# Paired attend steps in a masked attention, and cell edge projections placed ahead of the scores

## The chip, the cores and the metric

One core of one Trainium2 chip. The metric is the device time of one execution of the whole program, in microseconds (us). Before the change it is 3072.13 us, the median of three runs (3067.86 to 3075.75). Some 0.3% is what a measurement of this kernel can tell from no change.

## The reference, cut to what matters

The program takes `x`, 64 batches of 64 tokens by 256 features (4096 tokens), and runs six residual stages on it:

```
x = x + xattn0(layernorm(x), ctx, ctx, mask)     # "masked attention", 16 heads of 16
x = x + attn0(layernorm(x), context)             # "wide attention", 8 heads of 128, 1024 keys
x = x + ffn0(layernorm(x))                       # "cell": six nodes, each an attention
x = x + xattn1(layernorm(x), ctx)
x = x + attn1(layernorm(x))                      # a scan
x = x + ffn1(layernorm(x))
```

The change touches the first and the third. The masked attention projects queries from the normalised tokens, keys and values from the 256 context rows of each batch, closes masked keys, and takes a softmax over 256 keys per head. The cell computes six nodes in turn:

```
for c in range(6):
    q = ew[c,0] * (node[c-1] @ We[eq] + be[eq])          # the edge
    k = ew[c,1] * (node[snode] @ We[ek] + be[ek])
    v = ew[c,2] * (node[middle] @ We[ev] + be[ev])
    node[c] = act_w[c] * mha(q, k, v, Wq[c], Wk[c], Wv[c], Wo[c]) + q
out = layernorm(node[5])
```

Its attention has 8 heads of 32 and runs over the 64 tokens of one batch. Only node 0's value source (for node 1) is the node just computed; from node 2 on keys and values come from older nodes.

## The kernel before, in words

Every stage is a block in which each engine has its own instruction stream; a semaphore is raised by one engine and waited for by another. The order of the work is written out by hand: the functions named `body` list what each engine does in a unit, in order, and an engine never passes an instruction that waits.

**Masked attention** (`stage_masked_attention`, L447). 32 units of 128 tokens, that is two batches `b`, in a loop over two units (`units`, L545). A unit has 8 steps `t` (`STEPS`), each a pair of heads of one batch; the first four belong to batch 0, the last four to batch 1. Per unit PE does: `turn_probs(u, t)` (L750, matmuls L759) for all eight steps, into the one PSUM bank `turn`, so turn t waits until turn t-1 is copied; `scores` (L733, L745) for batch 1 of this unit and for batch 0 of the next; `attend(u, k, j)` (L762, L774) four times, j = 0 to 3, each from two steps' turned probabilities, tiles of 128*32; and for the next unit `project_q` (L690), `project_k` twice (L699, L709), `project_v` twice (L713, L722), plus `project_o` (L726) of the unit before and `turn_x` (L682) of the unit after the next. Its order (L778 to L819) is: turn 0, attend 3 of the unit before, queries, turn 1, scores batch 1, turn 2, attend 0, keys, turn 3, keys, turn 4, attend 1, output, turn 5, scores of the next unit, turn 6, attend 2, values, turn 7, values, turn_x.

Softmax: DVE adds the mask and finds the row minimum (`find_min`, L967), ACT takes the exponential with its row sum (`exp`, L883), DVE inverts the sum (`invert`, L1019), POOL multiplies (`scale_probs`, L637), PE turns, and ACT or DVE copies the turned block into `probT` (`copy_turned`, L892 and L977), which holds four steps, so the copy waits for an attend of the same unit. Every product of projections and scores is taken in three passes of high and low parts: ACT rounds the high part (`split_ctx` L859, `copy_q` L867, `copy_k` L872), DVE takes the low part (`ctx_lo` L981, `q_lo` and `k_lo` L984). POOL also normalises the tokens two units ahead (`inverse_std` L615, `normalise` L622 to L624), spreads the queries (`spread`, L629) and adds the bias (L643). DVE's `pick` (L1010, L1013) gathers the attended heads, `finish` (L1024) adds the output.

**Cell** (`stage_cell`, L1769). Four rounds `i`, each with two blocks of 512 tokens, the inputs X = 0 and 1. A round has twelve attentions: node c = 0 to 5, and for each X = 0, then 1. Attention number a = 12 i + 2 c + X. The PE order of one attention (L2192 to L2241) is: `add_edge(0, ...)` (first half of the edge projection, 6 matmuls of 512 columns into the bank `acc[0]`, L2137), `turn_late` (L2120, probabilities 2 and 3), `add_edge(1, ...)`, `attend` (L2148), keys of the next node for this X (L2063; in c = 0 only half of them here, in c = 5 `turn_input` L2052 instead), `add_output` (L2159), `turn_early` of the *other* input's probabilities 0 and 1 (L2112), values (L2086), queries (L2063 into `ring`), scores (L2101). So the scores of one X are computed while the other X is attended next.

DVE per attention (L2516 to L2557): for the four score banks row maximum and subtraction (L2465, L2468); in X = 0, after two of them, `split_fused` (L2412), the low part of the next fused weights, 128x1536; low part of the attended rows (L2413); sums, inversion and division of the probabilities (L2473, L2479, L2483); low part of the node (L2413); in X = 1 the low part of the own weights (`split_own`, L2449); in c = 3 and 4 the normalisation of the next round's input, in c = 5 `finish`, the last layernorm and the residual (L118 to L143, L2500, L2503). ACT copies turned probabilities, takes exponentials, rounds attended rows, keys, node, values and queries, splits the weights' high parts (L2266, L2271) and issues the loads of the next weights and the stores (`store`, L2330), each store waiting for `finish`. One semaphore, `set_lo`, counts both kinds of low weight parts. POOL in this stage only takes inverse square roots (`gpsimd_rstd`, L127).

## Time and profile before

| | |
|---|---|
| median of three runs | 3072.13 us (3067.86 to 3075.75) |
| the profiled execution | 3063.59 us, its span 3061.9 us |
| PE busy | 2868.9 us (94%) |
| DVE busy | 2214.2 us (72%) |
| ACT busy | 2050.7 us (67%) |
| POOL busy | 1104.2 us (36%) |
| first and last score matmul of the masked attention | 23.5 and 564.0 us |
| first and last edge matmul of the cell | 1632.7 and 2594.7 us |

A row of a timeline gives the start (us from the span's start), the length, the engine, the line, the operation with output<-inputs, the tile shape and operand shape of PE, and how many instructions were merged (x24). In brackets stands the idle time of the engine before the row and who ended it. Lengths of PE rows overlap a little, because matmuls are pipelined: the distance from start to start is what a group costs. "issue" is idle time for which the profile shows no other engine.

### The profile page before, as it was taken

Reading aid. Unit: us, or ns where it says so; the run is one execution under the profiler, and the core shown is the slowest. Engines: PE = TensorE matmul, PEld = TensorE weight load, DVE = VectorE, ACT = ScalarE, POOL = GpSimd, SP = SyncE. Lnnn points to the kernel's source line nnn. Section 1 sums busy time; section 2 is a strip of 40 time slices with the busy share of each in tenths; the row PEclk is TensorE's granted clock in tenths of the full one; section 3 lists DMA queues with packets and bytes.
Section 4 is the critical chain, followed back from the end, with each engine's and each line's share of the span. In section 5 each row is a group of like instructions: output and inputs, shape, how many; then the busy total and the mean of one; then the engine's idle time right before and its main releaser. Section 6 shows DMA issues by size and latency. Waiting matters only on the chain. (4 is left out here: it accounts for less than half of the span.)

```text
span 3061.9 us, 84828 instructions
## 1 busy us (share of the span) xinstructions
PE 2868.9 (94%) x32198; PEld 2227.6 (73%) x32198; DVE 2214.2 (72%) x5367; ACT 2050.7 (67%) x4144; POOL 1104.2 (36%) x939
## 2 busy tenths in 40 slices
PE   7999999789999999999979999999999998788899
PEld 6777777556666666666667887887887787566798
DVE  7888888777777767777637788788778776668543
ACT  6888888687777777787706766666676665333444
POOL 6777777476665555665600000000000000111210
PEclk9999999999999999999989999999999999899899
DMA  4111111077899888898961112111011110651000
GB/s 147 50 58 50 58 48 48 9 134 136 152 159 148 151 149 151 151 160 144 196 235 43 37 43 71 37 44 57 34 44 50 50 37 26 204 166 58 8 21 28
DMA packets 620992, 275.15 MB, mean 90 GB/s; under 512 B 548972, under 2 KB 593959, under 8 KB 620471
## 3 DMA queue, kind: packets, MB, share of 16 engines
q1 hardware_dynamic: 600726, 226.96, 35.0%
q10 hardware_dynamic: 19968, 44.05, 4.2%
q8 instruction: 208, 3.41, 0.5%
q14 instruction: 90, 0.73, 0.1%
HBM read 115.21 MB, written 21.50 MB: 45 GB/s over the span
## 5 line engine op out<-in xcount | busy, mean ns | idle before, releaser
L1334 POOL TENSOR_TENSOR front_parts<-wide_prob,front_parts 128x1024 f16<-128x1024 f32 x256 | 546.3, 2135 | 351.9 <-ACT front_parts L1555 278.8
L1653 DVE TENSOR_REDUCE wide_row_max<-wide_score 128x1 f32<-128x1024 f32 x256 | 312.6, 1221 | 130.0 <-PE wide_score L1375 129.8
L1543 ACT ACTIVATE wide_prob<-wide_score,wide_neg_max,wide_s_up 128x1024 f32<-128x1024 f32 x256 | 307.6, 1202 | 146.6 <-DVE wide_neg_max L1656 139.4
L1375 PE MATMUL wide_score<-wide_kT,wide_qT 128*128 128x512 f16 x1536 | 376.8, 382 | 6.5 <-ACT wide_prob L1543 4.9
L637 POOL TENSOR_TENSOR mask_prob<-mask_prob,mask_inv_sum 128x512 f32<-128x512 f32 x256 | 271.0, 1064 | 94.7 <-DVE mask_inv_sum L1019 90.8
L883 ACT ACTIVATE mask_prob<-mask_prob,mask_row_min 128x256 f32<-128x256 f32 x512 | 255.5, 502 | 68.3 <-DVE mask_row_min L967 64.9
L1555 ACT ACTIVATE front_parts<-wide_prob 128x1024 f16<-128x1024 f32 x256 | 269.9, 1054 | 16.9 <-ACT wide_prob L1543 8.7
L1375 PEld LDWEIGHTS wide_score<-wide_kT,wide_qT 128*128 128x128 f16 x1536 | 144.8, 98 | 154.3 <-ACT wide_prob L1543 6.6
L2465 DVE TENSOR_REDUCE cell_row_max<-cell_score 128x8 f32<-128x512 f32 x192 | 131.3, 684 | 152.5 <-PE cell_score L2101 149.9
L130 POOL TENSOR_TENSOR cell_var_eps<-cell_mean_var,const_eps 128x4 f32<-128x4 f32 x8 | 1.6, 202 | 641.2 <-DVE cell_mean_var L124 641.2
L1391 PE MATMUL wide_pv<-front_probT,wide_v 128*128 128x256 f16 x1536 | 188.8, 273 | 1.8 <-DMA front_probT<-front_parts 1.8
L1391 PE MATMUL wide_turn<-front_probT,wide_v 128*128 128x256 f16 x1536 | 188.3, 273 | 2.3 <-DMA front_probT<-front_parts 2.3
L967 DVE CUSTOM_DVE_ANT_0 mask_prob<-mask_score,mask_shut 128x256 f32<-128x256 f32 x512 | 189.4, 416 | 0.0
L1391 PEld LDWEIGHTS wide_pv<-front_probT,wide_v 128*128 128x128 f16 x1536 | 150.1, 98 | 45.7 <-issue 3.3
L1391 PEld LDWEIGHTS wide_turn<-front_probT,wide_v 128*128 128x128 f16 x1536 | 150.2, 98 | 45.5 <-issue 2.5
L759 PE MATMUL mask_turn<-const_ident,mask_prob 128*128 128x128 f32 x1024 | 158.4, 277 | 16.2 <-ACT mask_probT L892 13.3
L2137 PE MATMUL cell_acc<-cell_node,cell_w 128*128 128x512 f32 x576 | 160.3, 414 | 9.9 <-ACT cell_probT L2340 6.1
L2294 ACT ACTIVATE cell_v<-cell_score 64x256 f32<-64x256 f32 x384 | 145.5, 379 | 29.1 <-PE cell_score L2086 24.6
L2086 PE MATMUL cell_score<-cell_w,cell_node 128*128 128x256 f32 x1152 | 150.9, 288 | 5.5 <-DVE cell_node L2413 4.0
L130 POOL TENSOR_TENSOR cell_last_var_eps<-cell_last_mean_var,const_eps_cell 128x4 f32<-128x4 f32 x8 | 1.6, 202 | 420.2 <-DVE cell_last_mean_var L124 420.2
L2159 PE MATMUL cell_acc<-cell_oT,cell_w 128*128 128x512 f32 x576 | 145.3, 401 | 7.5 <-DVE cell_oT L2413 7.4
L759 PEld LDWEIGHTS mask_turn<-const_ident,mask_prob 128*128 128x128 f32 x1024 | 116.5, 141 | 46.3 <-POOL mask_prob L637 30.0
(356 smaller groups left out, 6848.7 us busy)
## 6 DMA issues: line engine op xcount, KB each, us to landing
cell_w_stage<-cell_weights ACTq DMA_DIRECT2D x24, 768.0 KB, 5.2
mask_ctx<-in_ctx_turned SPq DMA_DIRECT2D x32, 512.0 KB, 3.2
ctx_ctx<-in_ctx SPq DMA_DIRECT2D x32, 512.0 KB, 4.2
cell_w_stage<-in_L_ffn_W_own ACTq DMA_DIRECT2D x24, 512.0 KB, 3.6
mask_mask<-in_mask_BxS_ik SPq DMA_DIRECT2D x32, 256.0 KB, 3.5
front_probT<-front_parts SPq DMA_TRANSPOSE x512, 3.3
cell_prob<-in_L_ffn_W_pairs SPq DMA_DIRECT2D x10, 512.0 KB, 5.5
front_x_all<-in_x SPq DMA_DIRECT2D x32, 128.0 KB, 2.1
```

Source lines behind the costliest of these rows:

```text
L637: pool.tensor_tensor(prob[:, b, two, :], prob[:, b, two, :], inv_sum[:, b, two].unsqueeze(2).to_broadcast([P, 2, CTX]), ALU.mult)\
L759: mm = pe.transpose(turn[:, (i * KT + kt) * P:(i * KT + kt + 1) * P], prob[:, b, s * 2 + i, kt * P:(kt + 1) * P], ident[:, :])
L883: ins = act.activation(prob[:, b, p, :], prob[:, b, p, :], ACT.Exp, bias=row_min[:, b, p:p + 1], scale=-1.0, accum_out=row_sum[:, b, p:p + 1])
L967: ins = dve.tensor_tensor_reduce(prob[:, b, p, :], score[p % ROW][:, p // ROW * CTX:(p // ROW + 1) * CTX], shut[:, k, b, :], 1.0, 3.4e38, ...
L1334: pool.tensor_tensor(parts[:, s % 2, LO, :], prob[:, s % 2, :], parts[:, s % 2, HI, :], ALU.subtract).then_inc(part_lo, 1)
L1375: mm = pe.matmul(score[:, s % 2, half * 512:(half + 1) * 512], qT[:, u_par, a, s * P:(s + 1) * P], kT[:, par, b, half * 512:(half + 1) * 5 ...
L1391: mm = pe.matmul(pv_banks[hf][:, :], v[:, par, a, kb, :], probT[:, u_par, hf, :, b, kb, :], start=(kb == 0 and i == 0), stop=(kb == KB - 1 ...
L1543: act.activation(prob[:, s % 2, :], score[:, s % 2, :], ACT.Exp, bias=neg_max[:, s % 2:s % 2 + 1], scale=s_up[:, 0:1], accum_out=row_sum[: ...
L1555: act.activation(parts[:, s % 2, HI, :], prob[:, s % 2, :], ACT.Copy).then_inc(part_hi, 1)
L1653: dve.tensor_reduce(row_max[:, one], score[:, s % 2, :], AX.X, ALU.max).then_inc(max_found, 1)
L2086: mm = pe.matmul(score[2 + pair][:, s * D:(s + 1) * D], v_src[:, a, ih, half(2 * pair + s)], weight(b, fused_at(2), ih, slice(0, D)), star ...
L2137: pe.matmul(acc[oh][:, :], weight(a_, EDGE_AT, ih, half(oh)), src[:, b_, ih, :], start=(j == 0 and ih == 0), stop=False)
```

## The change

Masked attention: `probT` holds all eight steps; attends 0 and 1 stand together behind turn 4, attends 2 and 3 behind turn 0 of the next unit; ACT's exp 3 moves from the end of a unit behind `split_ctx` of the next; DVE's inversions 3 and 4 and POOL's scaling 7 change places with a neighbour. Cell: the first half of the next attention's edge projection stands between queries and scores; the low part of the fused weights moves from DVE to POOL, with a semaphore of its own; at the end of the last round `finish` and `store` of block 0 move behind the attended rows of the last attention.

```diff
-    probT = mem.sb("probT", [P, PER_BATCH, 2, KT, P])
+    probT = mem.sb("probT", [P, STEPS, 2, KT, P])
...
             scale_probs(u, 6)
+            scale_probs(u, 7)
             if not last and has_second(u):
                 inverse_std(u + 2)
                 normalise(u + 2, k)
-            scale_probs(u, 7)
...
+        def attend_batch(u, k, b):
+            for j in range(b * DH, (b + 1) * DH):
+                attend(u, k, j)
...
             turn_probs(u, 0)
             if not first:
-                attend(u - 1, 1 - k, GROUPS - 1)
+                attend_batch(u - 1, 1 - k, 1)
...
             turn_probs(u, 2)
-            attend(u, k, 0)
...
             turn_probs(u, 4)
-            attend(u, k, 1)
+            attend_batch(u, k, 0)
...
             turn_probs(u, 6)
-            attend(u, k, 2)
...
         def copy_turned(u, t):
             act.wait_ge(turn_ready, u * STEPS + t + 1)
-            if t >= PER_BATCH or positive(u):
-
-                act.wait_ge(heads_ready, u * GROUPS + t // 2 - 1)
+            if positive(u):
+
+                act.wait_ge(heads_ready, (u - 1) * GROUPS + t // 2 + 1)
...
             if not last:
                 split_ctx(u + 1, 1 - k)
+            exp(u, 3)
             copy_turned(u, 1)
...
                 copy_v(u + 1, 1 - k, 1)
-                exp(u + 1, 3)
...
-            invert(u, 3)
             if not last:
                 ctx_lo(u + 1, 1 - k)
+            invert(u, 3)
             find_min(u, k, 4)
...
             find_min(u, k, 5)
+            invert(u, 4)
             if not last and has_second(u):
                 ln_stats(u + 2, k)
-            invert(u, 4)
```

The cell, on POOL, PE, ACT and DVE in this order:

```diff
+        def split_fused(number):
+            pool.wait_ge(set_hi, number * 2 + 2)
+            pool.tensor_tensor(w_set[:, LO, FUSED_AT:SET], w_stage[:, FUSED_AT:SET], w_set[:, HI, FUSED_AT:SET].bitcast(F32), ALU.subtract)\
+                .then_inc(fused_lo, 1)
+
         def body(i, last):
-            for X in range(2):
-                if not last:
-                    norm.gpsimd_rstd(pool, (i + 1) * 2 + X)
+            for c in range(NODES):
+                if not (last and c == NODES - 1):
+                    split_fused(set_number(i, c))
+                if c in (3, 4) and not last:
+                    norm.gpsimd_rstd(pool, (i + 1) * 2 + c - 3)
...
         project_v(0, 1)
+        add_edge(0, 0, 0, 0, 1, 0)
         scores(DH, 2 * 6)
...
-                add_edge(0, a, c, X, set_no, use)
+                after = (c + X) % NODES if X == 1 else c
+                after_set = set_number(i, c) + X
+
+                def edge_ahead():
+                    add_edge(0, a + 1, after, 1 - X, after_set, use)
+
+                if final and X == 1:
+                    add_edge(0, a, c, X, set_no, use)
                 turn_late(use, a, X)
...
                     if X == 0:
-                        pe.wait_ge(set_lo, set_no * 2 + 2)
+                        pe.wait_ge(fused_lo, set_no + 1)
...
                     project_q(use + Q_AT, Q_AT, c + 1, X)
+                    edge_ahead()
                     scores(use + Q_AT, proj_at(i, c, X) + PROJ_SLOT)
...
                     project_q(use + Q_AT + DH, Q_AT + DH, 0, X)
+                    edge_ahead()
                     scores(use + Q_AT + DH, proj_at(i, c, X) + PROJ_LAST)
...
                     act.activation(oT[:, HI, hf, :], ring[hf][:, :], ACT.Identity, bias=fused_bias[:, c, 2, hf:hf + 1]).then_inc(attended_hi, 1)
+                if final and X == 1:
+                    store(i, 0)
...
-                    store(i, X)
+                    if not (final and X == 0):
+                        store(i, X)
...
-                if X == 0:
-                    if not final:
-                        split_fused(set_number(i, c))
...
                     low(oT[:, LO, hf, :], ring[hf][:, :], oT[:, HI, hf, :], fused_bias[:, c, 2, hf:hf + 1]).then_inc(attended_lo, 1)
+                if final and X == 1:
+                    finish(i, 0, last)
...
-                if c == NODES - 1:
+                if c == NODES - 1 and not (final and X == 0):
                     finish(i, X, last)
```

DVE's `copy_turned` changes as ACT's does. `set_lo` is split into `own_lo` (own weights, DVE) and `fused_lo` (fused weights, POOL); all waits on it follow.

## Rows read from the trace of the kernel before

**Rows 1.** windows view, masked, then cell: stretch, length, busy PE PEld DVE ACT POOL, clock, DMA

```profile
264.00:401.00 137.00, 132.86 (x1556) 107.05 (x1553) 115.20 (x472) 118.12 (x361) 105.99 (x120) 1.00 0.16 54
1850.00:2095.00 245.00, 236.13 (x4156) 196.75 (x4155) 195.92 (x337) 168.22 (x313) 4.84 (x8) 1.00 0.14 47
```

**Rows 2.** PE's timeline in a masked unit: start us, us, engine, line, operation

```profile
307.73 0.63 PE L759 MATMUL mask_turn<-const_ident,mask_prob 128*128 128x128 f32 x4 [0.33 <-ACT mask_probT L892]
308.29 0.64 PE L774 MATMUL mask_heads<-mask_probT,mask_v 128*32 128x128 f32 x16
308.86 1.66 PE L709 MATMUL mask_ring<-mask_ctxT,mask_w_kv 128*128 128x512 f32 x6
310.36 0.60 PE L759 MATMUL mask_turn<-const_ident,mask_prob 128*128 128x128 f32 x4
310.71 1.64 PE L709 MATMUL mask_ring<-mask_ctxT,mask_w_kv 128*128 128x512 f32 x6
...
315.23 0.98 PE L745 MATMUL mask_score<-mask_kT,mask_q_diag 32*128 32x256 f32 x24 [0.18 <-DVE mask_kT L984]
```

**Rows 3.** the weight loads (PEld) of attend in the same unit

```profile
308.29 0.38 PEld L774 LDWEIGHTS mask_heads<-mask_probT,mask_v 128*32 128x32 f32 x16 [0.17 <-issue]
```

**Rows 4.** ACT's timeline in the same unit

```profile
300.10 0.51 ACT L883 ACTIVATE mask_prob<-mask_prob,mask_row_min 128x256 f32<-128x256 f32 x1 [1.48 <-DVE mask_row_min L967]
...
309.29 0.51 ACT L883 ACTIVATE mask_prob<-mask_prob,mask_row_min 128x256 f32<-128x256 f32 x1 [0.30 <-DVE mask_row_min L967]
...
317.25 0.51 ACT L883 ACTIVATE mask_prob<-mask_prob,mask_row_min 128x256 f32<-128x256 f32 x1 [1.48 <-DVE mask_row_min L967]
```

**Rows 5.** DVE's timeline in the same unit

```profile
307.14 1.42 DVE L981 TENSOR_TENSOR mask_ctxT<-mask_ctx,mask_ctxT 128x1024 fp32r<-128x1024 f32 x1 [0.78 <-ACT mask_ctxT L859]
```

**Rows 6.** PE's timeline around one attention of the cell stage

```profile
1689.14 2.91 PE L2063 MATMUL cell_ring<-cell_node,cell_w 128*128 128x512 f32 x12
1691.98 1.76 PE L2101 MATMUL cell_score<-cell_kT,cell_qT 32*64 32x64 f32 x128
1693.67 1.65 PE L2137 MATMUL cell_acc<-cell_node,cell_w 128*128 128x512 f32 x6
...
1698.90 3.06 PE L2063 MATMUL cell_score<-cell_node,cell_w 128*128 128x512 f32 x12
...
1704.60 1.03 PE L2112 MATMUL cell_ring<-const_ident,cell_prob 128*128 128x128 f32 x8
...
1708.34 2.91 PE L2063 MATMUL cell_ring<-cell_node,cell_w 128*128 128x512 f32 x12
1711.54 1.58 PE L2101 MATMUL cell_score<-cell_kT,cell_qT 32*64 32x64 f32 x128 [0.30 <-ACT cell_qT L2286]
1713.06 1.65 PE L2137 MATMUL cell_acc<-cell_node,cell_w 128*128 128x512 f32 x6
```

**Rows 7.** DVE's timeline in and after the same attention

```profile
1699.67 1.41 DVE L2413 SCALAR_TENSOR_TENSOR cell_oT<-cell_ring,cell_fused_bias,cell_oT 128x512 fp32r<-128x512 f32 x2 [0.56 <-ACT cell_oT L2347]
...
1702.58 1.29 DVE L2483 TENSOR_TENSOR cell_prob<-cell_prob,cell_inv_sum 128x512 f32<-128x512 f32 x2
...
1715.77 1.75 DVE L2412 TENSOR_TENSOR cell_w<-cell_w_stage,cell_w 128x1536 fp32r<-128x1536 f32 x1
```

**Rows 8.** ACT's timeline at the end of it

```profile
1711.87 1.48 ACT L2271 ACTIVATE cell_w<-cell_w_stage 128x1536 fp32r<-128x1536 f32 x1
```

**Rows 9.** the page, part 5: the subtraction on POOL in the wide attention

```profile
L1334 POOL TENSOR_TENSOR front_parts<-wide_prob,front_parts 128x1024 f16<-128x1024 f32 x256 | 546.3, 2135 | 351.9 <-ACT front_parts L1555 278.8
```

**Rows 10.** the waits view of PE in the cell stage: us, times, longest

```profile
PE cell_acc L2159 <- DVE cell_oT L2413: 7.4, 9, 1.5
```

**Rows 11.** the end of the cell stage, PE's and DVE's timelines

```profile
2594.73 0.79 PE L2137 MATMUL cell_acc<-cell_node,cell_w 128*128 128x512 f32 x1 [6.09 <-ACT cell_probT L2340]
...
2606.41 1.41 DVE L118 BATCH_NORM_STATS2 cell_last_stats<-cell_z 128x6 f32<-128x256 f32 x4 [6.81 <-ACT cell_z L2374]
...
2612.38 1.23 DVE L2503 TENSOR_TENSOR cell_x_res<-cell_x_res,cell_z 128x1024 f32<-128x1024 f32 x1
```

More of the change, by code:

```diff
@@ L774, in attend @@
                     mm = pe.matmul(heads[r * ROWS:(r + 1) * ROWS, hf * P:(hf + 1) * P], v[:, k, b * KT + kt, p * ROWS:(p + 1) * ROWS],
-                                   probT[:, p // 2, p % 2, kt, :], start=(kt == 0), stop=(kt == KT - 1))
+                                   probT[:, b * PER_BATCH + p // 2, p % 2, kt, :], start=(kt == 0), stop=(kt == KT - 1))
             mm.then_inc(heads_ready, 1)
+        def attend_batch(u, k, b):
+            for j in range(b * DH, (b + 1) * DH):
+                attend(u, k, j)
         def body(u, k, first, last):
@@ L837, in _ @@
         units(pe, body)
-        attend(UNITS - 1, 1, GROUPS - 1)
+        attend_batch(UNITS - 1, 1, 1)
         pe.wait_ge(y_ready, UNITS - 1)
@@ L888, in copy_turned @@
             act.wait_ge(turn_ready, u * STEPS + t + 1)
-            if t >= PER_BATCH or positive(u):
-                act.wait_ge(heads_ready, u * GROUPS + t // 2 - 1)
-            act.activation(probT[:, t % PER_BATCH].rearrange("p i k q -> p (i k q)"), turn[:, :], ACT.Copy).then_inc(turn_copied, 1)
+            if positive(u):
+                act.wait_ge(heads_ready, (u - 1) * GROUPS + t // 2 + 1)
+            act.activation(probT[:, t].rearrange("p i k q -> p (i k q)"), turn[:, :], ACT.Copy).then_inc(turn_copied, 1)
         def body(u, k, first, last):
@@ L933, in _ @@
         exp(0, 2)
-        exp(0, 3)
         units(act, body)
@@ L973, in copy_turned @@
             dve.wait_ge(turn_ready, u * STEPS + t + 1)
-            if t >= PER_BATCH or positive(u):
-                dve.wait_ge(heads_ready, u * GROUPS + t // 2 - 1)
-            dve.tensor_copy(probT[:, t % PER_BATCH].rearrange("p i k q -> p (i k q)"), turn[:, :]).then_inc(turn_copied, 1)
+            if positive(u):
+                dve.wait_ge(heads_ready, (u - 1) * GROUPS + t // 2 + 1)
+            dve.tensor_copy(probT[:, t].rearrange("p i k q -> p (i k q)"), turn[:, :]).then_inc(turn_copied, 1)
         def low(dst, src, hi):
@@ L1847, in stage_cell @@
     set_hi = mem.sem("set_hi")
-    set_lo = mem.sem("set_lo")
+    own_lo = mem.sem("own_lo")
+    fused_lo = mem.sem("fused_lo")
     biases_done = mem.sem("biases_done")
@@ L2128, in add_edge @@
                 if X == 0:
-                    pe.wait_ge(set_lo, set_no * 2 + 1)
+                    pe.wait_ge(own_lo, set_no)
             src = node[:, X, :, place(source[c][0])]
@@ L2174, in _ @@
         turn_input(0, 0)
-        pe.wait_ge(set_lo, 2)
+        pe.wait_ge(fused_lo, 1)
         pe.wait_ge(proj_copied, DH)
@@ L2234, in body @@
                     if X == 0:
-                        pe.wait_ge(set_lo, set_no * 2 + 2)
+                        pe.wait_ge(fused_lo, set_no + 1)
                     pe.wait_ge(proj_copied, proj_at(i, c, X) + DH)
@@ L2376, in body @@
                 if X == 0 and not final:
-                    act.wait_ge(set_lo, set_number(i, c) * 2 + 2)
+                    act.wait_ge(own_lo, set_number(i, c))
+                    act.wait_ge(fused_lo, set_number(i, c) + 1)
                     load_set((c + 1) % NODES)
@@ L2423, in _ @@
                     dve.wait_ge(set_hi, 2)
-                    low(w_set[:, LO, FUSED_AT:SET], w_stage[:, FUSED_AT:SET], w_set[:, HI, FUSED_AT:SET]).then_inc(set_lo, 2)
-                    dve.wait_ge(set_lo, 2)
+                    low(w_set[:, LO, FUSED_AT:SET], w_stage[:, FUSED_AT:SET], w_set[:, HI, FUSED_AT:SET]).then_inc(fused_lo, 1)
+                    dve.wait_ge(fused_lo, 1)
             dve.tensor_scalar(edge_bias[:, c, :], be[:, :, edge[c][0]], ew_sb[:, 3 * c:3 * c + 1], None, ALU.mult)
@@ L2450, in split_own @@
                                                ALU.mult, ALU.subtract)
-            ins.then_inc(set_lo, 1)
-        def split_fused(number):
-            dve.wait_ge(set_hi, number * 2 + 2)
-            low(w_set[:, LO, FUSED_AT:SET], w_stage[:, FUSED_AT:SET], w_set[:, HI, FUSED_AT:SET]).then_inc(set_lo, 1)
+            ins.then_inc(own_lo, 1)
         def input_rest(blk, X, banks=score):
```

## The prediction

> **What bounds the kernel now.** I read the windows view first, then PE's timeline in the two stages the change touches, then the timelines of the engines that feed it, then PE's waits. In the masked attention PE is busy 132.9 of 137 us [rows 1], in the cell stage 236.1 of 245 us [rows 1]: both run at the pace of PE's instruction order, and only what shortens that order, or a wait inside it, pays. What the reader should see in each: how little PE idles, and that what it does wait for comes once per unit, at a fixed place.
>
> Masked attention. One unit lasts 17.15 us, from the exp of pair group 0 at 300.10 to the same at 317.25 [rows 4]. PE waits twice in it: 0.33 us before turn 2 (for ACT's copy of turn 1) and 0.18 us before the next unit's scores (for DVE's low part of the keys) [rows 2]. So the period is a loop over three engines: turn 2 (307.73) to the next scores (315.23), 7.50 us on PE [rows 2]; scores to exp 0 (317.25), 2.02 us by scores and row minimum [rows 2, 4]; exp 0 to turn 2, 7.63 us, whose pace ACT sets, since it is ACT's copy of turn 1 that PE waits for at its end [rows 2, 4].
>
> Cell. An attention takes 19.39 us here (1693.67 to 1713.06) [rows 6]. At its end come the queries, then the scores, which wait 0.30 us for ACT's copy of the queries; the scores then take 1.52 us. Where no wait is shown before them they take 1.69 us [rows 6], so I read 0.17 us of wait for the second query half inside them.
>
> **The change in the masked attention.** (1) Attend steps go in pairs. Turn 2 to attend costs 0.56 us and attend to keys 0.57, while turn 3 to keys costs 0.35 [rows 2]; taking attend 0 out from between turn 2 and keys saves 0.56 + 0.57 - 0.35 = 0.78 us, and the same again at turn 6. It comes back as the second attend of a pair. Its price is not shown: at most 0.57 us as now, at least the 0.38 us that its weight loads run, since 0.17 us of issue idle precedes each group [rows 3]. I take 0.45, nearer the lower end, because that idle stands where the tile shape changes (128*128 to 128*32) and nothing changes between two attends. By itself: the Trainium skill (TensorEngine Tiling (Array Packing), Key Properties) says that changing the tiling mode drains the engine and changing only the tile does not; by it the second attend costs the 0.38, by the row of a single attend 0.57, which is 6 us apart over the stage. (2) On ACT split_ctx goes ahead of exp 3; both stay before the copy of turn 1, so 7.63 us stays. But DVE's low part of the context, which now waits 0.78 us for ACT [rows 5], starts up to 1 us earlier, so row minima 4 follow the scores sooner, and the 0.30 us that ACT waits for them before exp 4 [rows 4] goes. (3) The copies into the doubled probT wait for an attend of the unit before: long done. (4) Scaling 7 moves ahead of POOL's normalisation, about 2.4 us of POOL work; PE needs the latter only at the end of the unit, about 1 us later than I place it. (5) The shut-off of attend 0 and 1 until turn 4 delays the pick into oT behind DVE work that waits for exp 7 anyway.
>
> PE's part of the loop: 7.50 - 0.78 + 0.45 - 0.18 (the wait) = 6.99; the keys' low part, ready at turn 2 + 7.3, comes 0.3 to 0.5 earlier, at 6.8 to 7.0: even. Scores to exp 0 and exp 0 to turn 2 unchanged. So 0.5 us a unit; with the row minimum also freed of 0.05, and a part of the second PE gain where turn 2 waited less, 0.55. Over 31 units: **17 us**. Bounds: 0.15 us a unit (second attend at 0.57, keys' low part moved by nothing), 5 us; and PE alone, 17.15 - 0.33 - 0.18 - 2 x (0.78 - 0.38) = 15.84, 1.3 us a unit, 40 us, which the ACT part of the loop excludes up to about 0.9, 28 us. Late next: PE now waits for ACT before turn 2 by 0.5 us or more.
>
> **The change in the cell.** Edge half 0 of the next attention goes between queries and scores: no instruction added. (1) It covers the query copies. Queries and scores take 3.20 + 1.52 = 4.72 us for this input and 2.84 + 1.69 = 4.53 for the other (1689.14 to 1693.67) [rows 6]; without waits 2.84 + 1.52 = 4.36. So 0.36 us for one and 0.17 for the other, and an attention takes 19.03 us in both. 32 plain attentions (cells 1 to 4 in four rounds): 16 x 0.36 + 16 x 0.17 = 8.5 us. (2) What the cover costs: scores to turn_early of the same scores' probabilities shrinks by the 1.49 us of edge 0. From the end of scores T, the first probabilities are ready on DVE at 1702.58 + 0.65 = T + 9.56, less the 0.56 us that DVE waited for ACT [rows 7], which attend, now 1.49 earlier, removes: T + 9.0. PE wants them at 1704.60 - 1693.67 - 1.49 = T + 9.44 [rows 6]. It holds, by 0.4. That is for input 1; for input 0 DVE has the low part of the fused weights in the same stretch, 1.75 us [rows 7], and there it would be late by 1.2 us: this is what moving it to POOL pays for. (3) On POOL: 1536 columns at 2.135 us per 1024 [rows 9] are 3.2 us. ACT has the high part ready at 1713.35, T + 0.3 [rows 8]; with 1.49 - 0.36 us put in ahead of T that becomes T - 0.8. So POOL ends at T + 2.4; keys need it at 1698.90 - 1693.67 - 1.49 = T + 3.74 [rows 6]. Hidden, margin 1.3 us. (4) Losses. DVE reaches the attended low part only at 1699.11 = T + 5.44 [rows 7], first half done at T + 6.1. In cell 0 only half the keys, in cell 5 only the input's turns stand ahead of add_output, which is then wanted at T + 5.2 and T + 4.7. Today these places wait 7.4 us in all [rows 10]. By my count input 1 loses 0.65 us in seven of them, 4.5 us, input 0, freed of 1.75 us of DVE, gains 0.3 to 1.0, 4 us: even. (5) The end. The last attention's half edge waits 6.09 us for ACT, which stands at the store of block 0 and that for DVE's finish [rows 11]. Now both come after the last attended copies. But finish 0 still takes 7.2 us (2606.41 to 2613.61 for the like one [rows 11]), the store still stands on ACT ahead of the last copies, and the second finish follows. It moves from 2606.4 to about 2603.4: 3 us, between 0 and 6. Cell: 8.5 + 0 + 3 = **11.5 us**, bounds 0 (scores to turns dearer by the 0.17 of a shape change, losses 8) and 20.
>
> **A rule that speaks against it.** The POOL subtraction at L1334 takes 2135 ns on average over 256 of them, beside a DVE that works too [rows 9], so I keep 3.2 us. By itself: the Trainium skill (GPSIMD Engine Reference, Key points) says GPSIMD shares its SBUF interfaces with VectorE and contends with DVE instructions that have two SBUF inputs; by it the subtractions after T would stretch POOL's pass. This is rival C.
>
> **Sum.** 17 + 11.5 = 28.5 us off. The profiled execution took 3063.6 us (span 3061.9), so 3035 by its own time. It stands 8.5 us, 0.28%, below the median of 3072.1, and below all three runs; the result is a median, so I take 3072.1 - 28.5, rounded to 3043.
>
> **Rivals.** A: the cell gives nothing, the DVE chain (0.4 us of margin) becomes its bound and the special cells lose; for it, the margins above; against, the 0.30 us waits of PE [rows 6]. Left: 17 - 3 = 14 us, 3058. B: the masked attention stays at 17.1 us, because another engine closes the loop, POOL above all (106 of 137 us busy [rows 1]) with scaling 0 behind the normalisation; left 11 to 13 us, 3060. C, slower: POOL's pass cannot run while DVE works. Place: keys of input 0. It decides once the pass takes more than 4.3 us. DVE works from T without pause to T + 5.4; POOL, with 2.4 us left at T, would end at T + 8 at the earliest, and the keys wait 4.2 us in 23 attentions, 97 us, less 25: 3144. Against it stand the POOL rows. D: both gain more, loop 0.9 us and cell 20 us: 48 us, 3024.
>
> **How the numbers follow.** Chances: forecast 0.60, A 0.12, B 0.10, C 0.04, D 0.10, nothing at all 0.04. A measurement of this kernel can tell some 0.3%, 9 us, from no change. A and B end at 3058 and 3060, close to the bound of 3063, and I give a part of each (0.08 together) to "same", with the 0.04 and a little of the forecast's tail: faster 0.83, same 0.12, slower 0.05. The range takes in A, B and nearly D: 3022 to 3064.
>
> **What would show it.** Right: the masked unit at 16.5 to 16.7 us with PE's wait before turn 2 grown to 0.5 us and none before scores; plain cell attentions at 19.0 to 19.1 us, no wait of scores for queries, none of keys for POOL; POOL's pass at 3.2 us; the 6.09 us wait gone and the last finish 3 us nearer. Wrong: keys waiting for POOL, turn_early waiting for DVE's probabilities, scores in the masked stage still waiting for the keys' low part, or the issue idles of PE grown, as dense short instructions of scores and attend now stand 1.5 us closer.

## The result, and the profile after

The changed kernel takes 3037.99 us (median of four runs, 3034.36 to 3042.38); the kernel before, beside it, 3072.92 (3067.86 to 3075.75). The ratio is 0.9892, 95% interval 0.9878 to 0.9906; a repetition (experiment 12) gave 0.9890 (0.9874 to 0.9906). So it is 1.1% faster, 33 us by the ratio and 35 by the medians; 28.5 were forecast. The profiled execution took 3038.47 us, its span 3036.8.

PE's waits in the masked attention, then in the cell stage and the start of the one behind it (us in total, times, longest):

```profile
PE mask_turn L759 <- ACT mask_probT L894: 6.7, 15, 1.8
PE mask_score L745 <- DVE mask_kT L985: 1.7, 1, 1.7
...
PE cell_acc L2168 <- DVE cell_oT L2436: 10.5, 12, 1.5
PE cell_ring L2157 <- issue: 6.6, 10, 1.1
PE cell_ring L2179 <- ACT cell_kT L2383: 6.4, 1, 6.4
...
PE cell_score L2072 <- POOL cell_w L2012: 2.2, 3, 0.8
...
PE cell_score L2110 <- issue: 1.2, 1, 1.2
```

The masked scores no longer wait for the keys in each unit (one wait of 1.7 us is left), and the cell's scores no longer wait for ACT's queries. The 6.09 us of [rows 11] has become 6.4 us one step later, at L2179. The output projection (`add_output`, L2168) waits for DVE 10.5 us in all, after the 7.4 us of [rows 10]. And the keys wait for POOL's pass three times, 2.2 us in all, in the cells 0 of the first, second and fourth round.

PE's timeline in a masked unit, to lay beside [rows 2]:

```profile
300.44 0.63 PE L759 MATMUL mask_turn<-const_ident,mask_prob 128*128 128x128 f32 x4
300.82 1.64 PE L709 MATMUL mask_ring<-mask_ctxT,mask_w_kv 128*128 128x512 f32 x6
302.30 0.60 PE L759 MATMUL mask_turn<-const_ident,mask_prob 128*128 128x128 f32 x4
302.65 1.64 PE L709 MATMUL mask_ring<-mask_ctxT,mask_w_kv 128*128 128x512 f32 x6
304.37 0.63 PE L759 MATMUL mask_turn<-const_ident,mask_prob 128*128 128x128 f32 x4
304.93 1.08 PE L774 MATMUL mask_heads<-mask_probT,mask_v 128*32 128x128 f32 x32
305.94 1.13 PE L730 MATMUL mask_ring<-mask_wT,mask_oT 128*128 128x256 f32 x4
...
307.44 0.98 PE L745 MATMUL mask_score<-mask_kT,mask_q_diag 32*128 32x256 f32 x24
...
317.09 0.63 PE L759 MATMUL mask_turn<-const_ident,mask_prob 128*128 128x128 f32 x4
```

The unit takes 16.65 us (300.44 to 317.09) instead of 17.15; turn 2 to scores 7.00 instead of 7.50. The pair of attends (x32) costs 1.01 us, a single one cost 0.57, so the second costs 0.44. But keys to turn 4, which is 1.47 us where nothing waits, takes 302.65 to 304.37, 1.72: an unshown wait of 0.25 us (no idle under 0.15 us stands in brackets in any row of this study, and an idle inside a merged row is not shown either; the distance from start to start shows both).

The cell, to lay beside [rows 6], PE's timeline, and POOL's new pass:

```profile
1698.14 2.91 PE L2072 MATMUL cell_ring<-cell_node,cell_w 128*128 128x512 f32 x12
1700.89 1.52 PE L2146 MATMUL cell_acc<-cell_node,cell_w 128*128 128x512 f32 x6
1702.34 1.59 PE L2110 MATMUL cell_score<-cell_kT,cell_qT 32*64 32x64 f32 x128
1703.87 1.09 PE L2129 MATMUL cell_ring<-const_ident,cell_prob 128*128 128x128 f32 x8
...
1707.70 3.06 PE L2072 MATMUL cell_score<-cell_node,cell_w 128*128 128x512 f32 x12
...
1721.34 1.59 PE L2110 MATMUL cell_score<-cell_kT,cell_qT 32*64 32x64 f32 x128
```

```profile
L2012 POOL TENSOR_TENSOR cell_w<-cell_w_stage,cell_w 128x1536 fp32r<-128x1536 f32 x23 | 79.9, 3473 | 639.7 <-ACT cell_w L2290 639.7
```

Queries, edge and scores follow each other with no idle in brackets, and an attention takes 19.0 us (1702.34 to 1721.34). POOL's pass is 3.47 us on average over 23.

### The profile page after: what moved, and what is told of

The parts are those of the page before. It is cut to its first block and busy times, and to the rows that moved or that the text cites. A ratio compares the mean times of both kernels' runs of the same rounds, so it can differ in the third digit from the quotient of the medians.

```text
span 3036.8 us, 84862 instructions
## 1 busy us (share of the span) xinstructions
PE 2852.6 (94%) x32198; PEld 2229.5 (73%) x32198; DVE 2174.6 (72%) x5344; ACT 2046.2 (67%) x4144; POOL 1174.6 (39%) x962
## 5 line engine op out<-in xcount | busy, mean ns | idle before, releaser
L2012 POOL TENSOR_TENSOR cell_w<-cell_w_stage,cell_w 128x1536 fp32r<-128x1536 f32 x23 | 79.9, 3473 | 639.7 <-ACT cell_w L2290 639.7
L885 ACT ACTIVATE mask_prob<-mask_prob,mask_row_min 128x256 f32<-128x256 f32 x512 | 254.9, 502 | 47.8 <-DVE mask_row_min L968 47.5
L759 PE MATMUL mask_turn<-const_ident,mask_prob 128*128 128x128 f32 x1024 | 157.7, 277 | 15.6 <-ACT mask_probT L894 6.7
L2146 PE MATMUL cell_acc<-cell_node,cell_w 128*128 128x512 f32 x576 | 154.1, 402 | 0.7 <-ACT cell_probT L2359 0.5
L2168 PE MATMUL cell_acc<-cell_oT,cell_w 128*128 128x512 f32 x576 | 144.8, 400 | 10.5 <-DVE cell_oT L2436 10.5
L2072 PE MATMUL cell_score<-cell_node,cell_w 128*128 128x512 f32 x576 | 147.4, 402 | 2.4 <-POOL cell_w L2012 2.2
```

The costliest lines, as they stand in the source:

```text
L759: mm = pe.transpose(turn[:, (i * KT + kt) * P:(i * KT + kt + 1) * P], prob[:, b, s * 2 + i, kt * P:(kt + 1) * P], ident[:, :])
L885: ins = act.activation(prob[:, b, p, :], prob[:, b, p, :], ACT.Exp, bias=row_min[:, b, p:p + 1], scale=-1.0, accum_out=row_sum[:, b, p:p + 1])
L2146: pe.matmul(acc[oh][:, :], weight(a_, EDGE_AT, ih, half(oh)), src[:, b_, ih, :], start=(j == 0 and ih == 0), stop=False)
```

## Where the gain lies: the profiles side by side

One profile is not enough here: the wide attention, the same code in all fourteen profiles, takes 983.1 to 991.6 us from the last group of masked score matmuls to the first matmul of the cell. The first column below is a mean over four profiles whose cell stage is that of before (before, experiments 1, 3 and 4), the second over four with the changed cell stage (the changed kernel, experiments 2, 6 and 12). The times run from the scores of one attention to those of the next and are added up (16 plain attentions of each input, which are those of the cells 1 to 4 in four rounds):

| us | cell as before (4 profiles) | changed (4 profiles) | edge in place (1) |
|---|---|---|---|
| plain, input 0 | 311.3 (309.4 to 312.8) | 309.4 (308.4 to 311.0) | 310.6 |
| plain, input 1 | 319.3 (317.6 to 320.1) | 306.1 (305.7 to 306.8) | 312.5 |
| cell 0, both inputs | 175.6 | 174.9 | 171.6 |
| cell 5, both inputs, three rounds | 136.2 | 136.7 | 135.0 |
| end of the last scores to the next stage's first matmul (two profiles each) | 49.6 | 47.4 | |

Plain attentions give 15.1 us, cells 0 and 5 nothing, the end 2.2: 17 us. The ranges of input 0 overlap, and three more profiles with these attentions (experiments 5, 10 and 11) give it 308.5 to 312.1 us, so that only the gain of input 1, 13 us, stands clear of what profiles of one kernel differ by. The last group of score matmuls of the masked attention starts 15.6 us earlier (563.4 in two profiles with the old stage, 547.8 on average in eight with the new one). Together that is 33 us, which is what the ratios say.

## The experiments

**1. The masked part alone**: the masked attention of the changed kernel, the cell stage of before (no other edit).

> The masked attention of the changed kernel, the cell stage of the kernel before. My theory: the two parts are separate and add up. The masked unit takes 16.65 us as in the changed kernel (17.15 before), PE waits before turn 0 and turn_x and no more before scores; 31 units give 16 us, of which the boundary to the wide stage takes back 2 to 3: 13 to 16 us below the kernel before. Rival: the stages interact (clock, boundaries), and this part brings all 35 us, or nearly nothing, when it stands alone.

Measured: 0.9954 (0.9940 to 0.9969), 14 us faster, as the theory said.

**2. The cell part alone**: the reverse.

> The cell stage of the changed kernel, the masked attention of the kernel before. My theory: 11 to 14 us below the kernel before; plain cell attentions 19.0 us against 19.3, POOL's pass 3.5 us, and the sum of this gain and that of the masked part alone is the whole gain of 35 us within 6 us. Rival: the parts interact, and the two gains miss the whole by over 10 us.

Measured: 0.9946 (0.9928 to 0.9964), 16.5 us faster. The two parts make 30.6 us of 33, and their intervals are 4 to 6 us wide either way: they add up as far as that tells. The cell's 16.5 us is over the 14 that I had given it at most.

**3. Pairs without the new orders** (the three engines' orders as before; the edit is shown against the masked part of the changed kernel):

```diff
-            scale_probs(u, 7)
             if not last and has_second(u):
                 inverse_std(u + 2)
                 normalise(u + 2, k)
+            scale_probs(u, 7)
...
                 split_ctx(u + 1, 1 - k)
-            exp(u, 3)
...
                 copy_v(u + 1, 1 - k, 1)
+                exp(u + 1, 3)
...
+            invert(u, 3)
             if not last:
                 ctx_lo(u + 1, 1 - k)
-            invert(u, 3)
```

(likewise the inversion of group 4 behind the layer norm statistics).

> Masked attention: attends in pairs and probT doubled, but the orders of ACT (exp 3 after the copy of values), DVE (inversions ahead of the context's low part) and POOL (normalisation ahead of scaling 7) as in the kernel before; cell stage as before. My theory: pairs shorten PE's order by 0.66 us a unit, but the keys' low part comes as late as before, so scores of the next unit wait for DVE by 0.2 to 0.4 us, and the unit takes 16.8 to 17.1 us: 2 to 11 us below the kernel before. Rival 1: the orders do not matter, the unit takes 16.65 us, 13 to 16 us below before. Rival 2: without the reorders nothing is gained, since the loop over ACT and DVE is what sets the unit.

Measured: 1.0011 (0.9999 to 1.0023), no gain; in its profile the last masked scores start at 568.1 us, 4.7 later than before. PE's waits in the masked attention:

```profile
PE mask_ring L709 <- DVE mask_ctxT L983: 10.3, 31, 1.0
PE mask_turn L759 <- POOL mask_prob L637: 9.6, 43, 0.4
```

and DVE's context row, to lay beside [rows 5]:

```profile
309.65 1.42 DVE L983 TENSOR_TENSOR mask_ctxT<-mask_ctx,mask_ctxT 128x1024 fp32r<-128x1024 f32 x1 [0.78 <-ACT mask_ctxT L861]
```

The unit takes 17.3 us (scores 300.59 to 317.88), which is rival 2. The wait is not where I expected it either, but once per unit at the keys' projection, which reads the context's low part, and [rows 5] show that part waiting for ACT. Without attend 0 between turn 2 and keys PE gets there 0.38 us after turn 2 starts and not 1.13, before the data, and the keys start at 0.95.

**4. The new orders without pairs** (the reverse of 3, on the kernel before: exp 3 behind split_ctx, inversions 3 and 4 and scaling 7 moved as in the change; attends one by one, probT of four groups).

> The kernel before with the changed orders of ACT, DVE and POOL in the masked attention, but attends one by one and probT as before; cell stage as before. My theory: PE's order stays 0.66 us longer, and the loop keeps its length but for what the keys' low part gains: PE no longer waits 0.18 us before scores, the unit takes 16.95 to 17.15 us, 0 to 6 us below the kernel before. Rival: the orders alone bring the unit to 16.65 us and pairs are worth nothing (13 to 16 us below).

Measured: 0.9956 (0.9943 to 0.9968), 13.5 us faster, as much as the whole masked change. PE's timeline:

```profile
300.21 0.63 PE L759 MATMUL mask_turn<-const_ident,mask_prob 128*128 128x128 f32 x4 [0.35 <-ACT mask_probT L892]
300.76 0.64 PE L774 MATMUL mask_heads<-mask_probT,mask_v 128*32 128x128 f32 x16
...
307.29 0.98 PE L745 MATMUL mask_score<-mask_kT,mask_q_diag 32*128 32x256 f32 x24
...
316.94 0.63 PE L759 MATMUL mask_turn<-const_ident,mask_prob 128*128 128x128 f32 x4 [0.35 <-ACT mask_probT L892]
```

The unit takes 16.73 us, turn 2 to scores 7.08 with every attend still in its place. My theory (16.95 us or more) falls, and the rival (16.65) holds but for 0.08 us.

**5. ACT's order taken back** in the changed kernel (the two exp edits of 3 alone).

> The changed kernel with ACT's order of the masked attention as before: exp 3 ahead of the high part of the context. The orders of DVE and POOL stay changed. In the run with pairs alone PE waited for DVE's low part of the context (10.3 us in 31 units) and for POOL's scaling (9.6 us). My theory: ACT's order is what counts, since the high part of the context, behind exp 3, is what DVE waits for; PE then waits 0.3 us before the values or keys that use the low part, the unit takes 17.1 to 17.3 us, and all of the masked part's gain is gone: 13 to 20 us above the changed kernel, PE waits on POOL under 3 us. Rival: POOL's order is what counts, and this kernel is within 5 us of the changed one.

Measured: 0.9929 (0.9915 to 0.9943), 12 us above the changed kernel, with some 6 either way. In the profile the last masked scores start at 561.2 us, so that 13.4 of the 15.6 us are gone. PE's timeline:

```profile
306.36 0.63 PE L759 MATMUL mask_turn<-const_ident,mask_prob 128*128 128x128 f32 x4
307.12 1.65 PE L709 MATMUL mask_ring<-mask_ctxT,mask_w_kv 128*128 128x512 f32 x6
```

Turn 2 to keys takes 0.76 us (0.38 in the changed kernel): PE waits for the context. The unit takes 17.07 us (scores 305.32 to 322.39). 12 us is just under the 13 that I expected at least, but ACT's order carries the masked gain; POOL's is tested next, and DVE's was taken back alone in no run.

**6. POOL's order taken back** (scaling 7 behind the normalisation, nothing else).

> The changed kernel with POOL's order of the masked attention as before: the normalisation of the unit after next ahead of scaling 7. My theory: scaling 7 comes 1.9 us later, turn 3 or turn 4 of the next unit waits for POOL by 0.2 to 0.4 us each unit (it was 9.6 us in all in the run with pairs alone); unit 16.8 to 17.0 us, 5 to 12 us above the changed kernel. Rival: with ACT's order changed POOL has slack for it, and the time is that of the changed kernel within 3 us.

Measured: 0.9899 (0.9883 to 0.9914), against 0.9890 for the changed kernel beside it: no difference. Two units take 33.31 us (scores 290.33 to 323.64), 16.66 each. Yet the waits view has one more line:

```profile
PE mask_turn L759 <- POOL mask_prob L637: 12.3, 31, 0.5
```

It is a wait of 0.4 us in every unit, at turn 7 and not at turn 3 or 4 as I had expected, and it costs nothing: in the changed kernel PE waits for ACT instead, 0.2 us before turn_x and 0.4 before turn 0 of the next unit, by the distances from start to start. The rival is right.

**7. The fused low part back on DVE**, behind its two subtractions of the row maxima:

```diff
                     subtract_max(a + 1, 1 - X, range(ROW // 2))
+                if X == 0 and not final:
+                    split_fused(set_number(i, c))
```

> The changed kernel with one thing taken back: DVE, not POOL, makes the low part of the fused weights, after its two subtractions of the row maxima. My theory: for input 0 the first probabilities then come 1.2 to 1.8 us after PE wants them, 23 times: turn_early waits 1.2 to 1.8 us for DVE in every second attention, 25 to 40 us above the changed kernel, 5 us below to 10 us above the kernel before. Rival 1: DVE has slack that I do not see and the time is that of the changed kernel. Rival 2: what is late is not the probabilities but the attended low part, so the wait stands before add_output and is under 0.5 us.

Measured: 0.9991 (0.9979 to 1.0003), 31 us above the changed kernel. Plain attentions of input 0 take 20.38 us in the median instead of 19.0. PE's timeline:

```profile
1698.83 1.49 PE L2150 MATMUL cell_ring<-cell_probT,cell_v 64*32 64x64 f32 x128
1701.02 3.00 PE L2065 MATMUL cell_score<-cell_node,cell_w 128*128 128x512 f32 x12 [0.70 <-DVE cell_w L2428]
1704.24 3.05 PE L2161 MATMUL cell_acc<-cell_oT,cell_w 128*128 128x512 f32 x12 [0.22 <-DVE cell_oT L2429]
1707.13 1.23 PE L2114 MATMUL cell_ring<-const_ident,cell_prob 128*128 128x128 f32 x8
```

It is 1.4 us, as the theory said, but not at turn_early alone: 0.7 us stand before the keys, which wait for the low part of the fused weights itself, 0.2 before the output projection, and the rest in turn_early and between the rows. DVE is late by its 1.75 us, and PE meets that in portions.

**8. Edge half 0 back in its place**, POOL's part kept:

```diff
-                if final and X == 1:
-                    add_edge(0, a, c, X, set_no, use)
+                add_edge(0, a, c, X, set_no, use)
...
-                    edge_ahead()
```

> The changed kernel with the first half of each edge projection back in its old place, behind the scores; POOL keeps the low part of the fused weights, and the end stays changed. My theory: scores wait again for ACT's copy of the queries, 0.36 us and 0.17 us in turn, 8.5 us over 32 plain attentions, and the cells are otherwise no faster: 6 to 12 us above the changed kernel. Rival: the gain of the cell came from taking 1.75 us off DVE, and this kernel is within 3 us of the changed one.

Measured: 0.9917 (0.9904 to 0.9931) against 0.9890, 8 us above the changed kernel with some 6 either way. The wait of the scores is back:

```profile
PE cell_score L2110 <- ACT cell_qT L2301: 5.3, 18, 0.8
PE cell_acc L2168 <- DVE cell_oT L2432: 4.2, 6, 1.5
```

The table above tells more than the sum. Plain attentions take 623.1 us, 7.5 less than with the cell before (630.6) and 7.6 more than in the changed kernel (615.5). Cells 0 and 5 take 306.6, 5.2 less than before (311.8) and 5.1 less than in the changed kernel (311.6). So POOL's part alone brings some 13 us, and the moved edge brings 7.6 in plain cells and costs 5.1 in cells 0 and 5, where the output projection then waits for DVE: 4.2 us against 10.5. So the rival has most of it by the traces: 12.7 of the cell's 15 us come with POOL's part, and the edge's net is 2.5. By the timed runs the edge is worth 8 us; the two intervals just overlap, and there is one profile on this side, so its size stays open between the two. The edge alone is a loss: with it and without POOL's part (experiment 7, 0.9991) the kernel is 11 us slower than with the cell of before (experiment 1, 0.9954). A kernel that moves the edge only in the plain cells might keep both gains; it was not tried.

What the two edits do in the plain cells differs. Take the attentions in which PE has no idle put to issue. For the inputs 0 and 1 their medians are 19.04 to 19.07 and 19.48 to 19.57 us with the cell of before, 19.05 and 19.53 here, 18.95 to 19.03 and 18.95 to 18.99 with the changed one. So the moved edge shortens these attentions, and POOL's part does not. What it brings here is that the long attentions of input 1, three or four of 16 with issue idles of up to 1.3 us in their scores, are gone; why they go is not shown.

**9. POOL's pass made twice**, the second behind the first:

```diff
+            pool.tensor_tensor(w_set[:, LO, FUSED_AT:SET], w_stage[:, FUSED_AT:SET], w_set[:, HI, FUSED_AT:SET].bitcast(F32), ALU.subtract)\
+                .then_inc(pool_once, 1)
+            pool.wait_ge(pool_once, number)
```

> The changed kernel with POOL's pass over the fused weights made twice, one behind the other, the same result each time. My theory: one pass of 3.5 us ends at T + 2.6 (T the start of turn_early), keys want it at T + 3.7; two end at T + 6.1 to T + 6.3, so keys of input 0 wait 2.4 to 2.6 us in some 20 attentions: 45 to 60 us above the changed kernel, 12 to 27 above the kernel before. Rival: the margin is larger than I read, or what keys lose is given back before the next attention, under 20 us above the changed kernel. A second rival, the condition of my rival C: the pass grows longer where DVE works beside it, to over 4 us.

Measured: 1.0104 (1.0086 to 1.0121), 66 us above the changed kernel, more than expected. PE's and POOL's timelines and PE's wait (us, times, longest), then the windows view of PE (stretch, length, busy with the number of instructions, granted clock, DMA share, GB/s):

```profile
1712.13 1.49 PE L2161 MATMUL cell_ring<-cell_probT,cell_v 64*32 64x64 f32 x128
1716.23 4.47 PE L2076 MATMUL cell_score<-cell_node,cell_w 128*128 128x512 f32 x12 [2.61 <-POOL cell_w L2016]
```

```profile
1709.08 3.47 POOL L2013 TENSOR_TENSOR cell_w<-cell_w_stage,cell_w 128x1536 fp32r<-128x1536 f32 x1 [35.16 <-ACT cell_w L2294]
1712.63 3.45 POOL L2016 TENSOR_TENSOR cell_w<-cell_w_stage,cell_w 128x1536 fp32r<-128x1536 f32 x1
```

```profile
PE cell_score L2076 <- POOL cell_w L2016: 46.6, 19, 4.3
```

```profile
1694.00:1713.00 19.00, 19.00 (x368) 1.00 0.01 3
1713.00:1717.00 4.00, 1.39 (x64) 0.87 0.01 4
1717.00:1721.00 4.00, 4.00 (x14) 0.70 0.00 0
```

The margin is as read: 3.5 us more on POOL make 2.5 us of wait, so 1.0 was spare. All 46 passes took 3.42 to 3.49 us, those beside DVE's work on the scores included, so the second rival falls. But such a wait can have a second price: behind this one PE runs its 12 key matmuls in 4.47 us instead of 3.06, and the granted clock is under full in both stretches that hold them. That is not so behind every wait:

```profile
1758.30 3.00 PE L2076 MATMUL cell_score<-cell_node,cell_w 128*128 128x512 f32 x12 [2.61 <-POOL cell_w L2016]
```

Of the 19 waits, ten are followed by slow key matmuls (granted clock 0.50 to 0.64 in the 4 us from their start) and nine, of 1.1 to 2.6 us, by matmuls at the usual pace (granted clock 1.00). By an estimate from these ten stretches of 4 us they lose 17 us of full speed, most of the 19 that are left of the 66 beside the 46.6 us of waiting.

**10 and 11. The store of block 0 late**, behind ACT's last copies of the node:

```diff
-                if final and X == 1:
-                    store(i, 0)
...
                             .then_inc(acc_copied, 1)
+                if final and X == 1:
+                    store(i, 0)
```

> The changed kernel, but at the very end ACT issues the store of block 0 behind its last copies of the node instead of ahead of them. My theory: the last PE wait of 6.4 us (for ACT, which stands at the store, which waits for DVE's finish of block 0) goes, and the end comes 2 to 5 us sooner: 0.1% below the changed kernel. Rival: DVE's finish of block 1, which stands behind finish 0, is what ends the stage, and nothing is gained.

> The changed kernel with the store of block 0 behind ACT's last copies of the node, once more, beside the changed kernel on the same chip. In its first profile the stretch from the last full scores to the first step of the context attention took 44.6 us against 47.5 in the changed kernel. My theory: 3 us, 0.1%, below the changed kernel, and not the 7 that the two ratios to the kernel before suggest. Rival: the store moved has a further effect, and it stays 6 us or more below.

Measured: 0.9868 (0.9850 to 0.9886), and in the repetition 0.9884 (0.9867 to 0.9900) beside 0.9890 for the changed kernel. PE's timeline at the end, the store late, then the changed kernel:

```profile
2560.96 3.05 PE L2168 MATMUL cell_acc<-cell_oT,cell_w 128*128 128x512 f32 x12 [1.50 <-DVE cell_oT L2436]
2564.78 1.09 PE L2179 MATMUL cell_ring<-const_ident,cell_kT 128*128 128x128 f32 x8 [0.78 <-ACT cell_kT L2381]
```

```profile
2570.57 3.06 PE L2168 MATMUL cell_acc<-cell_oT,cell_w 128*128 128x512 f32 x12 [1.50 <-DVE cell_oT L2436]
2580.08 1.97 PE L2179 MATMUL cell_ring<-const_ident,cell_kT 128*128 128x128 f32 x8 [6.44 <-ACT cell_kT L2383]
```

The wait of 6.44 us is 0.78. The stretch from the end of the last full scores to the next stage takes 44.5 and 44.6 us, against 47.5 and 47.3: 2.9 and 2.6 us. That is half of what the wait shrank by, and PE's wait at the start of the next stage grows from 16.3 to 19.9 us, behind DVE's second finish and the store. One profile with the old place of the store (experiment 6) takes 46.0 us: there the 12 matmuls of the output projection before the last took 3.06 us, behind a wait of 1.28. In the profiles of experiments 10 and 12 they took 4.6, behind waits of 1.6 and 1.5. The timed runs (7 us and 2 us) don't contradict 2.6 to 2.9, and don't show it: it is 0.1%. This kernel is the fastest of the study, by the place and not by its interval.

**12. The changed kernel once more**, as the measure.

> The changed kernel itself, as the measure for the runs around it on the same chip. Expected: 1.0 to 1.2% below the kernel before. In its profile the cell stage and the wide stage may each differ by up to 5 us from the first profile of it, by where the half clock falls; if they do, differences of under 10 us between single profiles are to be read from the places, not from the spans.

Measured: 0.9890 (0.9874 to 0.9906), span of the profile 3031.0 us against 3036.8 in the first. The same kernel differs by 5.8 us between two profiles: 1.4 up to the end of the masked attention, 2.0 in the wide one and 3.1 in the cell, less 0.7 behind it.

## Why the prediction was right, and which of its steps were not

**The total** (3043.0, measured 3037.99; 28.5 us off forecast, 33 to 35 measured) came out by two terms. The masked one has the right size for a reason that was not the real one, which is luck; the cell's is near the forecast in what it reasons on and has some 5 us on top that it did not foresee. (3072.1 - 28.5 is 3043.6, which I rounded the wrong way.) The profiled execution of before stood 8.5 us below the median, so the two spans differ by only 25 us.

**Masked attention: 17 us forecast, 15.6 in the traces.** The three parts of the loop came out at the forecast lengths: scores to exp 0 is 2.01 us, exp 0 to turn 2 7.64, turn 2 to scores 7.00 where I had 6.99. The second attend costs 0.44 us, where I took 0.45 between 0.38 and 0.57. What failed is the step "PE's part of the loop: 7.50 - 0.78 + 0.45 - 0.18". It took the 0.18 us shown as all the waiting in those 7.50. With the orders alone, and every attend in place, the stretch is 7.08, so 0.42 of it was waiting: keys to turn 4 took 1.57 us instead of 1.47, attend to output 0.63 instead of 0.58, turn 5 to scores 0.78 instead of 0.53, and only the last is marked, at 0.18 of its 0.25. PE's timeline of the kernel before, whose next row is the last of [rows 2], then of the orders alone:

```profile
314.45 0.60 PE L759 MATMUL mask_turn<-const_ident,mask_prob 128*128 128x128 f32 x4
```

```profile
306.76 0.60 PE L759 MATMUL mask_turn<-const_ident,mask_prob 128*128 128x128 f32 x4
307.29 0.98 PE L745 MATMUL mask_score<-mask_kT,mask_q_diag 32*128 32x256 f32 x24
```

So PE's own steps in the changed kernel make 7.08 - 0.78 + 0.45 = 6.75, and the 7.00 holds 0.25 of waiting, at turn 4. It waits for ACT's copy of turn 3, which ends at 304.22; POOL's scaling for turn 4 ends at 304.08. ACT's timeline of the changed kernel:

```profile
303.64 0.58 ACT L894 ACTIVATE mask_probT<-mask_turn 128x512 f32<-128x512 f32 x1
```

That the sum came to 6.99 all the same is luck: 0.24 us of waiting that it overlooked before stand against 0.25 us that it did not expect after. The clause on the other loop (the keys' low part ready at turn 2 + 7.3, coming 0.3 to 0.5 earlier), which I called even, was the one that carried the gain: it came at turn 2 + 7.26 before (314.99 against 307.73) and comes at + 6.69 now. The unit in us (over all 31 the means are 17.19 and 16.74, 17.34 and 16.68):

| | orders as before | orders changed |
|---|---|---|
| attends one by one | 17.15 | 16.73 |
| attends in pairs | 17.3 | 16.65 |

The exp of group 3 stood ahead of the context's high part on ACT, and DVE's low part, PE's keys and all that DVE does behind it hung on that; that move is worth 0.42 us a unit, and pairs 0.08 on top of it, but without it they cost 0.15. By "ACT sets the pace before turn 2" I predicted a wait of 0.5 us there. It is about 0.1: PE does wait for ACT, but earlier on that stretch, at turn_x and turn 0 (experiment 6).

**POOL** in the masked stage (rival B) does not close the loop: its order changes nothing (experiment 6).

**Plain cell attentions: 8.5 us forecast, 15.1 measured.** This is the term that was too small. Its mechanism was right for what it priced: scores no longer wait for queries, and an attention takes 18.99 us for 19.03 forecast. In the attentions without issue idles (experiment 8) two in a row fall from 38.6 us, as the two that I had read, to 38.0: some 10 us over the 32. The other 5 us I had at nothing. They are attentions of before that stood still at places put to issue, in the scores of all cells six times and up to 2.0 us each:

```profile
PE cell_score L2101 <- issue: 7.2, 6, 2.0
```

Over the four profiles on each side these idles in the scores went from 5.5 to 7.9 us to 0.8 to 1.2, those in attend from 2.7 to 3.8 to 4.4 to 6.6. I had feared that they would grow; in sum they fell by some 3 us, and experiment 8 shows that most of the fall in the scores comes with POOL's part and not with the edge. What these idles wait for stays open, and with it the cause of a third of this term.

**Cells 0 and 5: "even" forecast, 311.8 against 311.6 us.** This was right, and experiment 8 shows the two halves of it: 5.2 us won by DVE's relief, 5.1 lost by the moved edge. I had 4 and 4.5. What I did not see is that ACT has the high part ready later in a cell 0: there POOL's pass starts up to 4.8 us behind the start of the scores, in the plain cells 0.9, and three times the keys wait some 0.7 us for it. Keys waiting for POOL were one of my signs of being wrong; it is 2.2 us in all.

**DVE's chain and POOL's move.** The margin of 0.4 us for input 1 held (no wait of turn_early). That input 0 would be late by 1.2 us without POOL's move was 1.4 (experiment 7), though in other places than I wrote. POOL's pass was put at 3.2 us from the ratio of columns and takes 3.47: the price by column of [rows 9] (2.08 ns, here 2.26) did not carry over to another shape and another output type. The margin ahead of the keys was therefore 1.0 us, not 1.3, and experiment 9 measured it. Rival C had its place right and its threshold nearly (4.3 us; by experiment 9, 3.47 + 1.0), and its condition wrong.

**By itself:** the Trainium skill (GPSIMD Engine Reference, Key points) says that GPSIMD shares its SBUF interfaces with VectorE and contends with DVE instructions that have two SBUF inputs. Here nothing of that shows: the second passes of experiment 9, in which DVE is busy for some 3.4 us, took 3.45 us on average, and the first ones, most with 2.7 us, 3.47; a pass of the changed kernel in which DVE was busy for 1.3 us (at 2472.3) took 3.44.

**The end: 3 us forecast, 2.2 measured.** The wait of 6.09 us did not go, it moved to L2179, since the store that ACT stands at was still ahead of the copies that PE then needs. I had written that the store still stands ahead of the last copies, and costed it by DVE's finish; experiments 10 and 11 show the 2.6 to 2.9 us that were left there.

## What to carry to other kernels

When two edits come together, try each without the other: here the edit that looked like the gain (fewer switches on the busy engine) brought 0.08 us a unit, and a reordering on another engine 0.42. Before costing an engine's own steps, find its waits by comparing the distance from start to start at two places with the same work, and not by the marked idles alone: 0.24 of 0.42 us of waiting were unmarked. And take a repeated step's time from all its repetitions: the two attentions that I had read were of the usual length, and the long ones beside them held 5 of the 15 us of the plain cells.

## What the runs showed of the hardware

Behind ten of 19 PE waits of 1.1 to 4.3 us in the dense cell stage (experiment 9) the granted clock fell, in one of them to 0.50, the lower of its two levels (1.2 GHz, with 2.4 at full), for all of 4 us: 12 matmuls took up to 5.5 us instead of 3.0. Behind the other nine it stayed at 1.00, and up to 2.6 us the length of the wait does not tell the two kinds apart, since both have waits of 1.2 and of 2.6 us; the three of over 4 us are all of the first kind. In all, 46.6 us of waits cost 66. A wait that the trace shows in every unit (0.4 us, 31 times, experiment 6) can be free. And a stretch of short matmuls (107 of 128 scores, then 1.04 us of "issue") stops for no engine that the profile shows, up to 2.0 us at a time in the kernel before. PE's timeline of the kernel before:

```profile
2053.86 1.58 PE L2101 MATMUL cell_score<-cell_kT,cell_qT 32*64 32x64 f32 x107
2056.48 0.45 PE L2101 MATMUL cell_score<-cell_kT,cell_qT 32*64 32x64 f32 x21 [1.04 <-issue]
```

In which group of matmuls such idles fall went with the kernel: with the changed cell 1 us in scores and 4.4 to 6.6 in attend, with the edge in its old place 1.9 and 3.2, with the cell of before 5.5 to 7.9 and 2.7 to 3.8. What they wait for, no run here shows.
